# A vision transformer's tower on one core: attention contexts between a pair's two projections, value products ahead of the second pair, the shared expert's last unit in a third pair of banks, the merge behind three units

## The chip, the cores and the metric

The kernel runs on one core of a Trainium2 chip. Its engines are TensorE (PE, matrix products and transpositions into PSUM banks), VectorE (DVE), ScalarE (ACT), GpSimd (POOL) and SyncE (SP, which issues most transfers). Each follows its own instruction stream, and they meet at semaphores. The metric is the device time of one execution in microseconds (us), the median of three runs.

## The reference

The input is 16 images of 3x96x96, in float32 throughout. Cut to what matters:

```python
def tower(x):                                  # 16 images
    h = embed(x)                               # 36 patches of 16x16 -> 256, a class token, positions: (16, 37, 256)
    h = h + attention(layernorm(h))            # 16 heads of 64, relative position bias, softmax, w_o
    h = h + moe(layernorm(h))
    h = h + gated_scan(layernorm(h))           # s = (1 - d) s + d v with d = sigmoid(...), over the 37 tokens
    h = h + channel_mix(layernorm(h))          # sigmoid(xr W_r) * (relu(xk W_k)^2 W_v)
    return h

def attention(x):
    q, k, v = heads(x @ w_q), heads(x @ w_k), heads(x @ w_v)
    p = softmax(q @ k.T + bias)                # 37 x 37 for each image and head, no scaling
    return merge_heads(p @ v) @ w_o

def moe(x):                                    # 592 tokens, 7 experts of hidden width 1024
    top_vals, top_idx = top_k(x @ router_w.T, 2)
    combine = scatter(one_hot(top_idx) * softmax(top_vals))
    routed = [ (silu(x @ wg[e]) * (x @ wu[e])) @ wd[e] for e in range(7) ]
    shared = (silu(x @ swg) * (x @ swu)) @ swd
    return sum(combine[:, e] * routed[e]) + shared
```

## The kernel before, in words

**Layout.** The 592 tokens lie transposed, features on the 128 partitions, in two chunks (k) for the 256 features and two column halves (c) of 296 tokens, 8 images each. A product in nearly full float32 precision is three matmuls in a reduced type, high times high, low times high and high times low (`three`, L1673 to L1675). ACT makes the high part of an operand by a copy, DVE (`sub`, L1107) or POOL the low part by a subtraction. A product of 256 features for one column half and 128 outputs is thus 6 matmuls.

**Orders.** Every engine's order is written out by hand as one sequence of calls, and each call waits for semaphores by counts: `q_mm`/`k_mm` to `q_ev`/`k_ev` for projections and their copies, `sc_mm` to `sc_ev` for scores, `ctx_*` for contexts, `gate_mul` for multiplied hidden units, `dn_mm` for down products. PSUM banks are given by number; a writer waits until the last reader of the bank is through.

**Attention.** It goes over 8 pairs of heads; half t = 2p + c is pair p on images of column half c. Per half PE computes the scores of 8 images and 2 heads (L1809, 16 float32 matmuls, which the trace shows as 32), DVE adds the bias and takes the maxima (L1198, L1205), POOL subtracts them (`shift_scores`, L588), ACT takes the exponentials (L797), DVE sums and inverts (L1216, L1218), POOL normalises (L593), PE transposes the probabilities (`turn_probs`, L1824), ACT copies them (L792), and PE multiplies with the values (`contexts`, L1844), whose high and low parts ACT and DVE make (`context_high` L801, `context_low` through L1107). `project(p, c, j)` is a query (j = 0) or key (j = 1) projection, copied by ACT (`q_evac` L774, `k_evac` L782). In step p of the loop PE goes: scores of pair p, transpositions of pair p - 1, both projections of pair p + 1, contexts of pair p - 1, where a projection is the query or the key for both chunks of one column half. Values are five groups of token columns (`value(g, n)`, `v_evac` by ACT L749 or DVE L1165), part of which SP moves to other partitions by DMAs (L431). In step 0 there are no contexts; its place is taken by value groups 2 to 4, with the two projections of pair 1 among them.

Meanwhile SP fills buffers in DRAM (`fill_rows`, L474) and loads the experts' weights (`load`, L468), each behind a count of `sc_ev`.

**Shared expert.** It has 12 front units (FRONT), each 128 hidden features for one column half, and 4 back units that run ahead of the merge at the end of the MoE. A front unit is 12 matmuls of gate and up into the bank pair 0/1 or 2/3 by turns (`gate_up`), ACT's silu (L856), DVE's multiply (L1361), high and low parts (L863, L1107), and 12 down matmuls into banks that hold 8 units' sum for column half 0 and then 4 for half 1. Routing (top 2, places in the experts' lists) runs on DVE and POOL beside them, and POOL scatters rows by indirect DMAs (L621). `add_shared` (L1350) adds the down sums of a column half. Between the last two units PE transposes the gathered rows of expert 1 (`turn_rows`, L1965).

**Routed experts and merge.** Experts 1 to 7 take 224 gathered slots each (matmuls of 224 columns). The last one's output is scaled per slot into a high part (ACT L989) and a low part (DVE L1506), while fetched rows are weighted and summed (`scale_second` ACT L925, `weigh` DVE L1419). `merge(c)` (PE L2121 to L2129) multiplies the two parts by one-hot matrices and adds the weighted rows by an identity, each pair into one bank. The back units stand around it: two, `merge(0)`, the third, and so on, with `back_silu` (L914), `back_mul` (L1408), `back_high` (L919) on ACT and DVE.

Layer 1 (the gated scan and the channel mix) follows and is not touched.

## Time and profile before

| | |
|---|---|
| time, median of 3 runs | 312.22 us (310.87, 315.06, 312.22) |
| profiled execution's own time | 311.95 us |
| its span | 310.1 us |
| granted PE clock | 0.999 of full speed |
| PE busy, weight loads | 297.9 us (96%), 277.5 us (89%) |
| DVE, ACT, POOL busy | 189.7, 187.1, 158.1 us |

Times in the trace count from the span's start. Matmuls overlap, and their ends are modelled, so a row's busy time is longer than the step to the next one's start. The start of a row is firm; a gap between starts beyond the usual step is time that PE stood still, whether or not the row says idle. In brackets behind a row stand the idle time before it and what ended it.

### The profile page before, as it was taken

How to read it: one execution, taken by the hardware profiler on the slowest of the kernel's cores; microseconds unless marked ns; L12 is line 12 of the kernel's file. 1: busy time of each engine (PE TensorE's matmuls, PEld its weight loads, DVE VectorE, ACT ScalarE, POOL GpSimd, SP SyncE). 2: the span in 40 equal slices, each digit the busy share in tenths (PEclk: the TensorE clock that was granted, in tenths of full speed). 3: DMA queues.
4: the chain of work that ended last, by engine and by line, in shares of the span. 5: the costliest groups of instructions: out<-in, count | busy, mean ns of one | idle time of the engine just before them, and what ended most of it. 6: DMA issues, size and time to landing. Idle time of an engine off the chain costs nothing.

```text
span 310.1 us, 7379 instructions
## 1 busy us (share of the span) xinstructions
PE 297.9 (96%) x3082; PEld 277.5 (89%) x3082; DVE 189.7 (61%) x367; ACT 187.1 (60%) x326; POOL 158.1 (51%) x144
## 2 busy tenths in 40 slices
PE   8999998997999999999999999999999998999895
PEld 8877887996999999989999999999999998986673
DVE  2694445654645878467828775665748495746862
ACT  4485335774636793357697566657576463578661
POOL 7043613674535131746868495867685885100333
PEclk9999999999999999999999999999999999999999
DMA  7969343652422421669583838384856642000002
GB/s 260 406 161 232 63 113 96 206 159 71 139 61 77 128 95 48 212 188 284 171 267 127 264 117 285 107 285 147 269 169 235 200 156 87 22 2 2 1 0 82
DMA packets 32432, 46.49 MB, mean 150 GB/s; under 512 B 6965, under 2 KB 18837, under 8 KB 32394
## 3 DMA queue, kind: packets, MB, share of 16 engines
q1 hardware_dynamic: 29994, 42.16, 43.6%
q0 software_dynamic: 960, 2.43, 2.3%
q10 hardware_dynamic: 1440, 1.38, 1.5%
q8 instruction: 26, 0.43, 0.6%
q14 instruction: 12, 0.10, 0.1%
HBM read 38.22 MB, written 5.71 MB: 142 GB/s over the span
## 4 chain that ended last, share of the span: by engine, by line
PE 82%; DVE 8%; ACT 3%; issue 2%; DMA 2%; another core or an unknown queue 1%; SPq 0%; ACTq 0%; POOL 0%; DVEq 0%; POOLq 0%
PE ps L1673 20%; PE ps L1675 20%; PE ps L1674 19%; PE ps L2055 6%; PE ps L1844 3%; PE ps L1695 3%; PE ps L1824 2%; PE ps L1688 2%; DMA v_region<-v_region 2%; PE ps L1809 1%; PE ps L1681 1%; PE ps L1703 1%; DVE c_region L1107 1%; DVE w_lo L1107 1%
## 5 line engine op out<-in xcount | busy, mean ns | idle before, releaser
L1673 PE MATMUL ps<-c_region,w_hi 128*128 128x224 f32 (+2 forms) x304 | 88.2, 290 | 0.8 <-DVE c_region L1107 0.8
L1675 PE MATMUL ps<-c_region,w_lo 128*128 128x224 f32 (+2 forms) x304 | 85.4, 281 | 0.0
L1674 PE MATMUL ps<-c_region,w_hi 128*128 128x224 f32 (+2 forms) x304 | 85.2, 280 | 0.0
L565 POOL TENSOR_TENSOR w_lo<-w_stage,w_hi 128x512 fp32r<-128x512 f32 x30 | 48.6, 1638 | 34.1 <-ACT w_hi L834 34.0
L1673 PEld LDWEIGHTS ps<-c_region,w_hi 128*128 128x128 f32 x304 | 58.1, 191 | 1.6 <-DVE c_region L1107 1.0
L1674 PEld LDWEIGHTS ps<-c_region,w_hi 128*128 128x128 f32 x304 | 58.1, 191 | 0.3
L1675 PEld LDWEIGHTS ps<-c_region,w_lo 128*128 128x128 f32 x304 | 58.1, 191 | 0.0
L834 ACT ACTIVATE w_hi<-w_stage 128x1024 fp32r<-128x1024 f32 (+1 forms) x42 | 49.7, 1195 | 2.6 <-DVE v_region L1519 2.6
L1107 DVE TENSOR_TENSOR c_region<-s_region,c_region 128x448 fp32r<-128x448 f32 (+1 forms) x44 | 37.4, 851 | 17.5 <-ACT c_region L961 11.6
L572 POOL TENSOR_TENSOR w_lo<-w_stage,w_hi 128x512 fp32r<-128x512 f32 x28 | 38.0, 1389 | 8.2 <-ACT w_hi L834 8.2
L1673 PE MATMUL ps<-xn_split,w_hi 128*128 128x296 f32 x128 | 39.8, 311 | 0.6 <-DVE xn_split L1107 0.4
L1675 PE MATMUL ps<-xn_split,w_lo 128*128 128x296 f32 x128 | 38.2, 298 | 0.0
L1674 PE MATMUL ps<-xn_split,w_hi 128*128 128x296 f32 x128 | 38.2, 298 | 0.0
L1675 PE MATMUL ps<-w_hi,c_region 128*112 128x256 f32 (+2 forms) x120 | 34.6, 288 | 0.0
L1674 PE MATMUL ps<-w_lo,c_region 128*112 128x256 f32 (+2 forms) x120 | 34.5, 288 | 0.0
L1673 PE MATMUL ps<-w_hi,c_region 128*112 128x256 f32 (+2 forms) x120 | 34.5, 288 | 0.0
L1107 DVE TENSOR_TENSOR w_lo<-w_stage,w_hi 128x1024 fp32r<-128x1024 f32 x24 | 32.7, 1362 | 1.4 <-ACT w_hi L713 1.1
L961 ACT ACTIVATE c_region<-s_region 128x448 fp32r<-128x448 f32 x28 | 16.2, 578 | 20.2 <-DVE s_region L1467 19.4
L1467 DVE TENSOR_TENSOR s_region<-s_region,ps 128x448 f32<-128x448 f32 x28 | 17.2, 615 | 17.5 <-ACT s_region L956 17.1
L1673 PEld LDWEIGHTS ps<-xn_split,w_hi 128*128 128x128 f32 x128 | 24.2, 189 | 1.5 <-issue 0.6
L1674 PEld LDWEIGHTS ps<-xn_split,w_hi 128*128 128x128 f32 x128 | 24.1, 189 | 0.1
L1675 PEld LDWEIGHTS ps<-xn_split,w_lo 128*128 128x128 f32 x128 | 24.2, 189 | 0.0
(183 smaller groups left out, 565.5 us busy)
## 6 DMA issues: line engine op xcount, KB each, us to landing
w_stage<-in_w_gate SPq DMA_DIRECT2D x17, 512.0 KB, 4.3
w_stage<-in_w_up SPq DMA_DIRECT2D x17, 512.0 KB, 4.5
w_stage<-in_w_down SPq DMA_DIRECT2D x7, 1024.0 KB
expert_rows<-blank_rows SPq DMA_DIRECT2D x4, 448.0 KB, 5.1
v_region<-in_blocks SPq DMA_DIRECT2D x6, 272.0 KB, 4.1
w_stage<-in_w_down SPq DMA_DIRECT2D x3, 512.0 KB
v_region<-expert_rows SPq DMA_DIRECT2D x1, 1344.0 KB, 8.6
expert_out<-v_region ACTq DMA_DIRECT2D x6, 224.0 KB, 4.0
```

Of the source, the lines that this page charges most:

```text
L565: w = g.tensor_tensor(wl[:, r], ws[:, r], wh[:, r].bitcast(F32), ALU.subtract)
L572: w = g.tensor_tensor(wl[:, r], ws[:, r], wh[:, r].bitcast(F32), ALU.subtract)
L834: a.activation(piece(wh, n, rows), piece(ws, n, rows), ACT.Copy).then_inc(hi_e[n], 1)
L961: a.activation(gh_h[:, i * G:(i + 1) * G], prod_g[:, (i % 2) * G:(i % 2 + 1) * G], ACT.Copy).then_inc(s["g_hi"], 1)
L1107: return v.tensor_tensor(o, x, hi.bitcast(F32), ALU.subtract)
L1467: v.tensor_tensor(pat(prod_g, (i % 2) * G, [SLOTS, 2], [1, SLOTS]), pat(silu_g, (i % 2) * G, [SLOTS, 2], [1, SLOTS]), pat(bank(2 * (i % 2) ...
L1673: mm(o, a_h, b_h, start=start, stop=False)
L1674: mm(o, a_h, b_l, start=False, stop=False)
L1675: return mm(o, a_l, b_h, start=False, stop=stop)
L1695: w = mm(var_bank(L, c), ones[:], sq[:, k * N + c * NC:k * N + (c + 1) * NC], start=(k == 0), stop=(k == KD - 1))
L1844: w = mm(ps[64 * hd:64 * hd + 64, b0 + b, o:o + T], v_all[k_, vo + hd * DH:vo + (hd + 1) * DH], ptb[k_, po:po + T], start=True, stop=True)
L2055: w = mm(o, last_w(w_i, k, m), x[:, k * width + o0:k * width + o0 + NC], start=(k == 0), stop=(k == KD - 1))
```

## The change

Nothing is added to or taken from the arithmetic. The orders, the waits and some banks change:

- In steps 1 to 6 of the attention loop both contexts of pair p - 1 stand between the two column halves of pair p + 1's projections, and no longer behind the second half. `q_evac` and `k_evac` of that second half stand behind both `context_high` on ACT.
- The first column half of pair 1's projections is computed beside pair 0's, in banks 4 and 5, and all value groups 2, 3 and 4 stand ahead of the second half. Their copies are spread between the exponentials (ACT) and the sums (DVE). On POOL the low half of the query weights' later columns goes behind pair 0's two `shift_scores`.
- SP's fills and first down-weight loads wait for `k_ev` at 8, 10, 12, 14 and 16 in place of `sc_ev` at 6, 8, 10, 12 and 14.
- Unit 10 of the shared expert goes to banks 6 and 7, and unit 11 to banks 0 and 1. PE then transposes expert 1's rows (now into bank 2) and runs the down products of units 8 to 11 together. ACT and DVE take two pieces of expert 1's weights ahead of unit 8, and DVE's two adds stand behind the low parts.
- `merge(0)` stands behind three back units, and inside it the wait for the weighted rows (`mixed`) stands behind the one-hot products. ACT's first two `back_silu` and DVE's first two `back_mul` move ahead.

```diff
...
-    return bank(0, G) if e == 1 else pat(bank(4), D, [512, KD], [1, SLOTS])
+    return bank(2, G) if e == 1 else pat(bank(4), D, [512, KD], [1, SLOTS])
...
+def unit_bank(u):
+    return (6, 0)[u - FRONT + 2] if u >= FRONT - 2 else 2 * (u % 2)
...
-    return 4 if n == 1 else 6
+    return 4 if n == 2 else 6
...
     load("g0", 0)
-    sp.wait_ge(s["sc_ev"], 6)
+    sp.wait_ge(s["k_ev"], 8)
...
     load("u0", 0)
-    sp.wait_ge(s["sc_ev"], 8)
+    sp.wait_ge(s["k_ev"], 10)
...
     load("g1", 0)
-    sp.wait_ge(s["sc_ev"], 10)
+    sp.wait_ge(s["k_ev"], 12)
...
     for i in range(2):
-        sp.wait_ge(s["sc_ev"], 12 + 2 * i)
+        sp.wait_ge(s["k_ev"], 2 * HP - 2 + 2 * i)
...
-    for p in (2, 1, 0):
+    def columns_low(p):
...
+    columns_low(2)
+    columns_low(1)
...
         shift_scores(2 * p + 1)
+        if p == 0:
+            columns_low(0)
...
-    def q_evac(n):
+    def q_evac(n, done=None):
         hp, c = n // 2, n % 2
-        act.wait_ge(s["q_mm"], n + 1)
+        act.wait_ge(s["q_mm"], (n if done is None else done) + 1)
...
-    for n in range(2):
-        q_evac(n)
-        k_evac(n)
+    q_evac(0)
+    k_evac(0)
+    q_evac(2, 1)
+    q_evac(1, 2)
+    k_evac(1)
+    k_evac(2)
...
-    q_evac(2)
+    v_evac(2)
     exponentials(0)
-    k_evac(2)
+    v_evac(3)
     exponentials(1)
-    v_evac(2)
-    v_evac(3)
+    v_evac(4)
...
     k_evac(3)
-    v_evac(4)
...
             exponentials(2 * p + 1)
+        context_high(2 * p - 2)
+        context_high(2 * p - 1)
...
             output_high(p - 2)
-        context_high(2 * p - 2)
-        context_high(2 * p - 1)
...
             act.wait_ge(s["gate_mul"], done + (u - 1))
-        a.activation(silu_b[:, (u % 2) * NC:(u % 2 + 1) * NC], bank(2 * (u % 2), NC),
+        b = unit_bank(u) if isinstance(e, int) and e == 0 else 2 * (u % 2)
+        a.activation(silu_b[:, (u % 2) * NC:(u % 2 + 1) * NC], bank(b, NC),
...
-    for u in range(FRONT):
+    def rows_high(e):
+        act.wait_ge(s["xg_mm"], e)
+        a.activation(xg(e)[0], turned(e), ACT.Copy).then_inc(s["g_xh"], 1)
+    for u in range(KH):
...
             shared_high(u)
-        if u in (7, 8):
-            piece_high(("g0", "u0")[u - 7], 1)
+    piece_high("g0", 1)
+    piece_high("u0", 1)
+    silu(0, KH)
+    for u in range(KH + 1, FRONT):
+        silu(0, u)
+        shared_high(u - 1)
+    rows_high(1)
+    shared_high(FRONT - 1)
...
-    def rows_high(e):
-        act.wait_ge(s["xg_mm"], e)
-        a.activation(xg(e)[0], turned(e), ACT.Copy).then_inc(s["g_xh"], 1)
-    rows_high(1)
...
                                  scale=slot_w[0:SP, st:st + 1]).then_inc(s["yw_hi"], 1)
+                back_silu(0)
                 scale_second(2)
+                back_silu(1)
...
             gathered_expert(e)
-        back_silu(0)
-        back_silu(1)
...
             context_low(2 * p - 3)
-        if p < HP:
+        if p == 0:
+            v_evac(2)
+            sums(0)
+            v_evac(3)
+            sums(1)
+            v_evac(4)
+        elif p < HP:
...
             sums(2 * p + 1)
-        if p == 0:
-            for g in (2, 3, 4):
-                v_evac(g)
...
     rank_experts(0, TA)
-    for u in range(FRONT):
+    def shared_mul(u):
...
             dve.wait_ge(s["hid_lo"], u - 1)
-        v.tensor_tensor(prod_b[:, r], silu_b[:, r], bank(2 * (u % 2) + 1, NC),
+        v.tensor_tensor(prod_b[:, r], silu_b[:, r], bank(unit_bank(u) + 1, NC),
                         ALU.mult).then_inc(s["gate_mul"], 1)
+    for u in range(KH):
+        shared_mul(u)
...
             late_rows()
-        if u == 8:
-            piece_low("g0", 1)
-        if u == 10:
-            dve.wait_ge(s["dn_mm"], KH)
-            add_shared(0, s["acc_ok"])
-            add_shared(1, s["acc_ok"])
+    piece_low("g0", 1)
+    shared_mul(KH)
+    for u in range(KH + 1, FRONT):
+        shared_mul(u)
+        shared_low(u - 1)
...
     rows_low(1)
+    shared_low(FRONT - 1)
     piece_low("g1", 1)
+    dve.wait_ge(s["dn_mm"], KH)
+    add_shared(0, s["acc_ok"])
+    add_shared(1, s["acc_ok"])
...
                                            op1=ALU.subtract).then_inc(s["yw_lo"], 1)
+                back_mul(0)
                 weigh(2)
-                back_mul(0)
+                back_mul(1)
...
-        back_mul(1)
...
         n = 2 * hp + c
-        if n >= 2:
+        if n not in (0, 2):
...
             project(0, c, j)
+        project(1, 0, c)
...
         hp, half = t // 2, t % 2
-        pe.wait_ge(s["q_ev"], t + 1)
+        pe.wait_ge(s["q_ev"], 3 if t == 1 else t + 1)
...
         if p + 1 < HP:
-            project(p + 1, 0, 0)
-            project(p + 1, 0, 1)
             if p == 0:
-                for g in (2, 3):
+                for g in (2, 3, 4):
...
                         value(g, n)
+            else:
+                project(p + 1, 0, 0)
+                project(p + 1, 0, 1)
+                contexts(2 * p - 2)
+                contexts(2 * p - 1)
...
             project(p + 1, 1, 1)
-            if p == 0:
-                for n in range(2):
-                    value(4, n)
...
             output(1, 0, 0, 4)
-        if p >= 1:
...
         c, j = unit(u) if shared else (u // KH, u % KH)
-        if not (shared and u < 2):
-            pe.wait_ge(s["gate_mul"], u - 1 if shared else e * 16 + (u - 1 - BACK))
+        if not shared:
+            pe.wait_ge(s["gate_mul"], e * 16 + (u - 1 - BACK))
+        elif u == FRONT - 2:
+            pe.wait_ge(s["xt_ok"], 3)
+            pe.wait_ge(s["count_set"], 1)
+        elif u >= 2:
+            pe.wait_ge(s["gate_mul"], u - 2 if u == FRONT - 1 else u - 1)
+        b = unit_bank(u) if shared else 2 * (u % 2)
...
                 x_ = slice(k * NT + c * NC, k * NT + (c + 1) * NC)
-                w = three(bank(2 * (u % 2) + q, NC), wh[:, w_], wl[:, w_], xh[:, x_], xl[:, x_],
+                w = three(bank(b + q, NC), wh[:, w_], wl[:, w_], xh[:, x_], xl[:, x_],
...
             pe.wait_ge(s["d_x1"], 16)
-            pe.wait_ge(s["gate_mul"], FRONT - 1)
+            pe.wait_ge(s["gate_mul"], FRONT - 2)
...
             for st in range(ST):
-                o = bank(0, SP, k * SLOTS + st * SP) if e == 1 else bank(4 + k, SP, D + st * SP)
+                o = bank(2, SP, k * SLOTS + st * SP) if e == 1 else bank(4 + k, SP, D + st * SP)
...
             pe.wait_ge(lo_e["dn"], 1)
-        if u == KH + 2:
-            pe.wait_ge(s["xt_ok"], 3)
-            pe.wait_ge(s["count_set"], 1)
-        if u == FRONT - 1:
-            turn_rows(1)
-        down(0, u - 2, first=u - 2 in (0, KH))
+        if u < FRONT - 2:
+            down(0, u - 2, first=u == 2)
...
             turn_tokens(u - 3)
-    down(0, FRONT - 2)
-    down(0, FRONT - 1)
+    turn_rows(1)
+    pe.wait_ge(s["gate_mul"], FRONT - 1)
+    for u in range(KH, FRONT):
+        down(0, u, first=u == KH)
...
             pe.wait_ge(s["yw_lo"], ST)
-            pe.wait_ge(s["mixed"], TT if c else 3)
...
                     mm(bank(o, NC), yw_l[0:SP, y_], hot(st, c)[0:SP, :], start=False, stop=False)
-                t, k0, k1, at = PART[c]
-                mm(bank(o, k1 - k0, at), back0[:, t * D + m * P:t * D + (m + 1) * P], ident[:, k0:k1],
+            pe.wait_ge(s["mixed"], TT if c else 3)
+            t, k0, k1, at = PART[c]
+            for m in range(KD):
+                mm(bank(4 + 2 * c + m, k1 - k0, at), back0[:, t * D + m * P:t * D + (m + 1) * P], ident[:, k0:k1],
...
         back_gate_up(1)
+        back_gate_up(2)
         merge(0)
-        back_gate_up(2)
...
```

Three places of the orders. The first is PE in the attention loop, at the end of the second half's key projection and what follows, up to the scores of the next pair (`ps` is a PSUM bank; one float32 matmul here is two in the trace). Before:

```order
L1673 MATMUL ps<-xn_split,w_hi 128x296 [waits k_ev]
L1674 MATMUL ps<-xn_split,w_hi 128x296
L1675 MATMUL ps<-xn_split,w_lo 128x296
L1673 MATMUL ps<-xn_split,w_hi 128x296
L1674 MATMUL ps<-xn_split,w_hi 128x296
L1675 MATMUL ps<-xn_split,w_lo 128x296
L1844 MATMUL ps<-probs_T,v_region 64x37 [waits ctx_lo,pt_ev]
L1844 MATMUL ps<-probs_T,v_region 64x37 x15
L1844 MATMUL ps<-probs_T,v_region 64x37 [waits pt_ev]
L1844 MATMUL ps<-probs_T,v_region 64x37 x15
L1809 MATMUL ps<-k_buf,q_buf 37x37 [waits sc_ev,k_ev,q_ev]
L1809 MATMUL ps<-k_buf,q_buf 37x37 x15
```

And now:

```order
L1697 MATMUL ps<-xn_split,w_hi 128x296 [waits k_ev]
L1698 MATMUL ps<-xn_split,w_hi 128x296
L1699 MATMUL ps<-xn_split,w_lo 128x296
L1697 MATMUL ps<-xn_split,w_hi 128x296
L1698 MATMUL ps<-xn_split,w_hi 128x296
L1699 MATMUL ps<-xn_split,w_lo 128x296
L1834 MATMUL ps<-k_buf,q_buf 37x37 [waits sc_ev,k_ev,q_ev]
L1834 MATMUL ps<-k_buf,q_buf 37x37 x15
L1834 MATMUL ps<-k_buf,q_buf 37x37 [waits k_ev,q_ev]
L1834 MATMUL ps<-k_buf,q_buf 37x37 x15
```

The 32 context matmuls no longer stand between the key projection and the scores that read its copy.

The second place is DVE at the end of the shared units (multiply, low part, weight pieces, the two adds). Before:

```order
L1361 TENSOR_TENSOR s_region<-s_region,ps 128x296 [waits hid_lo,hid_hi,silu_ok]
L1107 TENSOR_TENSOR c_region<-s_region,c_region 128x296 [waits dn_mm,hid_hi]
L1107 TENSOR_TENSOR w_lo<-w_stage,w_hi 128x2x512 [waits hi_g0]
L1361 TENSOR_TENSOR s_region<-s_region,ps 128x296 [waits hid_lo,hid_hi,silu_ok]
L1107 TENSOR_TENSOR c_region<-s_region,c_region 128x296 [waits dn_mm,hid_hi]
L1361 TENSOR_TENSOR s_region<-s_region,ps 128x296 [waits hid_lo,hid_hi,silu_ok]
L1107 TENSOR_TENSOR c_region<-s_region,c_region 128x296 [waits dn_mm,hid_hi]
L1350 TENSOR_TENSOR hT<-hT,ps 128x296 [waits dn_mm]
L1350 TENSOR_TENSOR hT<-hT,ps 128x296
L1361 TENSOR_TENSOR s_region<-s_region,ps 128x296 [waits hid_lo,hid_hi,silu_ok]
L1107 TENSOR_TENSOR c_region<-s_region,c_region 128x296 [waits dn_mm,hid_hi]
L1107 TENSOR_TENSOR c_region<-ps,c_region 128x448 [waits g_xh]
```

And now:

```order
L1122 TENSOR_TENSOR w_lo<-w_stage,w_hi 128x2x512 [waits hi_g0]
L1379 TENSOR_TENSOR s_region<-s_region,ps 128x296 [waits hid_lo,hid_hi,silu_ok] x2
L1122 TENSOR_TENSOR c_region<-s_region,c_region 128x296 [waits dn_mm,hid_hi]
L1379 TENSOR_TENSOR s_region<-s_region,ps 128x296 [waits hid_lo,hid_hi,silu_ok]
L1122 TENSOR_TENSOR c_region<-s_region,c_region 128x296 [waits dn_mm,hid_hi]
L1379 TENSOR_TENSOR s_region<-s_region,ps 128x296 [waits hid_lo,hid_hi,silu_ok]
L1122 TENSOR_TENSOR c_region<-s_region,c_region 128x296 [waits dn_mm,hid_hi]
L1122 TENSOR_TENSOR c_region<-ps,c_region 128x448 [waits g_xh]
L1122 TENSOR_TENSOR c_region<-s_region,c_region 128x296 [waits dn_mm,hid_hi]
L1122 TENSOR_TENSOR w_lo<-w_stage,w_hi 128x2x512 [waits hi_g1]
L1368 TENSOR_TENSOR hT<-hT,ps 128x296 [waits dn_mm]
L1368 TENSOR_TENSOR hT<-hT,ps 128x296
```

The weight piece moved ahead of unit 8's multiply, each multiply now precedes the low part of the unit before, and the adds went to the end.

The third place is DVE ahead of the merge (yw low parts, weighted row, back units). Before:

```order
L1506 SCALAR_TENSOR_TENSOR c_region<-ps,softmax_stats,c_region 112x256 [waits yw_hi,slot_ok,g_y]
L1506 SCALAR_TENSOR_TENSOR c_region<-ps,softmax_stats,c_region 112x256 [waits yw_hi]
L1419 SCALAR_TENSOR_TENSOR v_region<-v_region 128x256 [waits r_scaled,d_back2]
L1408 TENSOR_TENSOR s_region<-probs_T,ps 128x296 [waits b_silu]
L1107 TENSOR_TENSOR w_lo<-w_stage,w_hi 128x1024 [waits hi_dn]
L1408 TENSOR_TENSOR s_region<-probs_T,ps 128x296 [waits b_silu]
```

And now:

```order
L1530 SCALAR_TENSOR_TENSOR c_region<-ps,softmax_stats,c_region 112x256 [waits yw_hi,slot_ok,g_y]
L1530 SCALAR_TENSOR_TENSOR c_region<-ps,softmax_stats,c_region 112x256 [waits yw_hi]
L1432 TENSOR_TENSOR s_region<-probs_T,ps 128x296 [waits b_silu]
L1443 SCALAR_TENSOR_TENSOR v_region<-v_region 128x256 [waits r_scaled,d_back2]
L1432 TENSOR_TENSOR s_region<-probs_T,ps 128x296 [waits b_silu]
L1122 TENSOR_TENSOR w_lo<-w_stage,w_hi 128x1024 [waits hi_dn]
```

The first back unit's multiply now stands ahead of `weigh`, the second right behind it.

## Rows read from the trace of the kernel before

**Rows 1.** The page, parts 1 and 3: busy time, and PE's instruction queue

```profile
PE 297.9 (96%) x3082; PEld 277.5 (89%) x3082; DVE 189.7 (61%) x367; ACT 187.1 (60%) x326; POOL 158.1 (51%) x144
...
q8 instruction: 26, 0.43, 0.6%
```

**Rows 2.** Table of waits, PE: total us, times, longest us

```profile
PE ps L1824 <- issue: 2.6, 1, 2.6
```

**Rows 3.** Timeline of PE, pair 0: start, us, line, operation, [idle before <-releaser]

```profile
27.52 0.30 PE L1675 MATMUL ps<-xn_split,w_lo 128*128 128x296 f32 x1
28.21 0.41 PE L1673 MATMUL ps<-xn_split,w_hi 128*128 128x296 f32 x1 [0.39 <-DVE xn_split L1107]
...
30.05 0.49 PE L1809 MATMUL ps<-k_buf,q_buf 64*37 64x37 f32 x32
30.72 0.49 PE L1809 MATMUL ps<-k_buf,q_buf 64*37 64x37 f32 x32 [0.18 <-ACT k_buf L782]
31.14 0.41 PE L1673 MATMUL ps<-xn_split,w_hi 128*128 128x296 f32 x1
```

**Rows 4.** Timeline of ACT, the same stretch

```profile
30.16 0.42 ACT L782 ACTIVATE k_buf<-ps 128x296 f32<-128x296 f32 x1 [0.39 <-PE ps L1675]
```

**Rows 5.** Timeline of PE, steps 4 and 5 of the loop

```profile
62.63 0.82 PE L1809 MATMUL ps<-k_buf,q_buf 64*37 64x37 f32 x64
63.38 1.02 PE L1824 MATMUL ps<-consts,s_region 101*111 101x101 f32 x8
64.18 0.38 PE L1673 MATMUL ps<-xn_split,w_hi 128*128 128x296 f32 x1
...
67.61 1.14 PE L1844 MATMUL ps<-probs_T,v_region 37*64 37x37 f32 x64
68.56 0.82 PE L1809 MATMUL ps<-k_buf,q_buf 64*37 64x37 f32 x64
71.96 0.99 PE L1824 MATMUL ps<-consts,s_region 101*111 101x101 f32 x8 [2.58 <-issue]
```

**Rows 6.** Timeline of DVE, the same stretch

```profile
63.51 0.47 DVE L1198 TENSOR_TENSOR s_region<-ps,bias_pair 101x296 f32<-101x296 f32 x1 [1.85 <-PE ps L1809]
...
65.26 0.83 DVE L1107 TENSOR_TENSOR c_region<-ps,c_region 128x296 fp32r<-128x296 f32 x2
```

**Rows 7.** Windows: length, PE, PEld, DVE, ACT, POOL busy, clock, DMA share, GB/s

```profile
67.40:69.40 2.00, 1.98 (x131) 1.70 (x129) 0.19 (x1) 1.52 (x4) 1.50 (x3) 1.00 0.56 186
69.40:70.60 1.20, 0.00 (x0) 0.00 (x0) 1.13 (x3) 0.14 (x1) 0.72 (x2) 1.00 0.06 17
```

**Rows 8.** DMA queues from 69.40 to 70.60: packets, MB, share

```profile
q8 instruction: 1, 0.02, 4.8%
```

**Rows 9.** Timelines of DVE and PE, values and contexts of pair 0

```profile
43.19 0.69 DVE L1165 COPY v_region<-ps 128x512 f32<-128x512 f32 x1 [3.70 <-PE ps L1675]
...
48.24 0.67 PE L1844 MATMUL ps<-probs_T,v_region 37*64 37x37 f32 x32
50.27 0.67 PE L1844 MATMUL ps<-probs_T,v_region 37*64 37x37 f32 x32 [1.36 <-DMA v_region<-v_region]
```

**Rows 10.** Timelines of ACT and PE, end of the shared units

```profile
131.94 0.42 ACT L856 ACTIVATE s_region<-ps 128x296 f32<-128x296 f32 x1 [2.47 <-PE ps L1675]
...
132.90 0.41 PE L1673 MATMUL ps<-xn_split,w_hi 128*128 128x296 f32 x1 [0.19 <-issue]
...
140.09 0.40 PE L1673 MATMUL ps<-c_region,w_hi 128*128 128x296 f32 x1 [0.76 <-DVE c_region L1107]
...
141.02 0.34 PE L1673 MATMUL ps<-c_region,w_hi 128*128 128x224 f32 x1
```

**Rows 11.** Timelines of ACT, DVE and PE ahead of the merge

```profile
262.14 0.84 ACT L989 ACTIVATE c_region<-ps,softmax_stats 112x256 fp32r<-112x256 f32 x2 [4.31 <-remote]
...
262.74 0.88 DVE L1506 SCALAR_TENSOR_TENSOR c_region<-ps,softmax_stats,c_region 112x256 fp32r<-112x256 f32 x2 [3.77 <-ACT c_region L989]
...
264.16 0.37 PE L2121 MATMUL ps<-xn_split,c_region 112*128 112x296 f32 x1 [1.38 <-DVE v_region L1419]
```

## The prediction, made from the rows of the kernel before alone

> **What bounds the kernel now.** I read the page first: the tensor engine (PE) is busy 297.9 of 310.1 us [rows 1], so only what PE waits for can move the time. Next the table of waits, which puts PE's largest idle time ahead of a transposition of the probabilities, 2.6 us with no releaser [rows 2]; the next, 1.38 us, is ahead of the merge [rows 11]. Since the ends of matmuls are modelled, I then took the starts of PE's instructions in the timeline: projection matmuls start every 0.14 us, and a longer step is a stall even where it reads as busy. So read, these are what the change can reach: 0.55 us at 28.21 (0.69 us after the start before it, not 0.14) [rows 3]; about 0.34 us in pair 0, where 64 score matmuls take 30.05 to 31.14 = 1.09 us against 62.63 to 63.38 = 0.75 us later [rows 3, 5]; 1.57 us between the contexts of pair 0's halves, 48.24 to 50.27 (half of 64 take 0.48) [rows 9]; 2.58 us at 69.38 to 71.96; 0.76 us and more at the end of the shared units [rows 10]; 1.5 us before the merge [rows 11]. All else runs packed, at a granted clock of 1.00 [rows 7].
>
> **The attention loop.** No matmul is added. The contexts of the pair before move from behind the second projections to between the first and the second. In a packed loop that saves nothing; what matters is which covers go.
>
> (1) The key projection of a pair is now followed at once by the next pair's scores. Their first half needs old buffers only, their second half this projection's copy by ACT. Pair 0 of the old kernel has exactly this order: projection ends, first scores at 30.05, ACT copies k 30.16 to 30.58 [rows 4], second scores 30.72. So the second half starts 0.67 us after the first and not 0.33: +0.34 us. Before, 0.95 us of contexts (67.61 to 68.56) hid that copy. It now comes ahead of pairs 1 to 7. Pair 1's is counted in (4): 6 x 0.34 = +2.0 us. Bounds: 0.18 (what the row itself calls idle) and 0.40 each, 1.1 to 2.4.
>
> (2) The contexts write banks that DVE must have read for the pair before (the low halves, L1107, awaited as ctx_lo). DVE does that at 65.26 to 66.09, 2.6 us after its start at 63.51, which is 0.13 us behind the scores [rows 5, 6]. Old contexts started at 67.61, 1.5 us later. Counted from the first scores T: scores now end T+1.09, DVE starts T+1.22 and is done T+3.80; PE has transpositions (0.80) and two projections (64.18 is 0.80 after 63.38; half of 64.18 to 67.61 = 1.7) behind it and stands ready at T+3.6 to 3.7. It waits 0.2 us, and one more change between kinds of matmul costs 0.08 (64.18 starts a matmul that takes 0.22 to the next). 5 pairs (2 to 6) x 0.28 = +1.4 us; bounds 0 (DVE starts behind the first half) and 0.5 each, 0 to 2.5. Queued behind the waiting contexts are the second projections and the next scores, so it is paid in full.
>
> (3) The stall at 69.38. Nothing that PE waits for is late: it stands with no releaser. In the 1.2 us from 69.40 PE does nothing, the data queues nearly stop (DMA share 0.56, then 0.06) [rows 7], and one packet of PE's instruction queue moves [rows 8]. That queue moved 26 packets in all for 3082 matmuls and as many weight loads [rows 1]: 237 instructions each. Contexts and scores back to back, 67.61 to 69.38, are 128 matmuls and 128 loads, over one packet's worth in 1.77 us. I read it as the instruction stream running dry where this stretch met a packet's edge while a fill of expert_rows and a weight load held the queues. Two projections now stand inside the stretch (1.6 us, and 0.34 of wait), and the fills are issued behind the pair's last copy and not with the load. I take -2.3 us of the 2.58; bounds 0 and -2.58.
> By the Trainium skill's page "Runtime: NRT & Kernel Launch", section "Instruction fetch mechanics", the crossing of a 16 KiB block is mostly hidden, since dispatch is slower than the fill. By that rule the stall is no fetch and has no reason to leave, and the sum below would be 313.6. The row of 2.58 us with no releaser speaks against "hidden"; the rule stands as rival B.
>
> (4) Pairs 0 and 1. A first projection of pair 1 in each column half fills the 0.55 us at 28.21 and covers the copy of pair 0's keys (0.34). All three value groups now run ahead of pair 1's second projections, so the last value copy (43.19 to 43.88 [rows 9]) comes some 2 us earlier, and with it the two transfers behind it, which let the contexts go at 50.27. But the contexts wait earlier too, by 1.6 us. I give that wait 0.35 us back (bounds 0 and 1.57), 0.2 for the transpositions that waited for the last value copy, take 0.4 off because group 3 needs a gather whose issue does not move, and 0.34 off for pair 1's scores. Sum -0.7, less 0.2 for changes of kind: -0.5 us; bounds +0.3 and -1.8.
>
> ACT and DVE have the same instructions per pair. POOL's part of the query weights goes behind two shifts; its readers are the projections of pairs 4 to 7. SP's fills wait for k_ev in place of sc_ev, most of a pair later; what they and the loads behind them bring is read only behind the loop. All that costs nothing as long as PE's loop stays the longest.
>
> **The shared units.** Old: ACT takes unit 8's silu at 131.94 though its matmuls ended near 129.5, and ends up behind; the last multiply stands behind the two adds, so the last down matmuls start 140.09 with 0.92 us lost (0.76 of it idle), and 0.35 us goes ahead of 132.90 [rows 10]. New: unit 10 goes to banks 6 and 7, so unit 11 follows with no wait, the four last down groups go together, and the adds stand behind. Even with silu 8 at 131.94: units 10 and 11 end 136.0, the rows' transposition follows (4 matmuls, 0.3), four down groups of 0.81 end at 139.7; the last low half is ready by 138.6 (silu 11 at 136.15, then 0.42, 0.46, 0.45, rows 0.53, then 0.50, with the handovers). Expert 1 starts 139.75 and not 141.02: -1.25 us; bounds 0 (the wait is only passed on) and -1.3 (all of it). The experts behind show no idle PE, so it is kept.
>
> **The merge.** A third back unit goes ahead of it. But it reuses banks 0 and 1, so it needs back_mul(0), which needs back_silu(0), which stands behind ACT's scaled copies. They start only at 262.14 [rows 11]. Then ACT 0.84, DVE's two low parts to 263.62, back_mul(0) to 264.1: the unit starts at 264.15, and the merge started at 264.16. The cause, the late copy, stays; only the last link changes. I take 0, bounds +0.4 and -1.5.
>
> **Sum** against the profiled execution's 311.95 us: -0.5 +2.0 +1.4 -2.3 -1.25 +0 = -0.65, so 311.3. The median of the three runs is 312.22, 0.27 above; I forecast **311.4 us**, that is, no difference that can be told.
>
> **Rivals.** A, as summed: 0.42, own range 310.2 to 312.8. B, the other side: the instruction stall stays or strikes at another edge, while waits (1) and (2) come. It decides at a packet's edge near the first contexts of pair 4 or 5. 311.4 + 2.3 = 313.7, slower than before; for it: the fetch needs some 2.5 to 4 us (71.96 - 67.61 = 4.35 at most) and the new stretch lasts only 3.7; 0.22. C, the waits do not come (DVE starts sooner, ACT's copy is hidden): 311.4 - 3.4 = 308.0; against it pair 0's rows; 0.14. D, the merge's wait of 1.5 us is hidden because ACT's copies come early: 309.9; 0.10. E, the end of the units gains nothing (a late silu of a later unit): 312.6; 0.07. Left over 0.05.
>
> The range from **307.8 to 314.8** holds A to E and the bounds of (1) to (4) around B and C. 2% of 312.22 is 6.2 us, about what a measurement here can tell from none: faster by that would need every stall gone and no new wait, 0.04; slower would need stalls of over 6 us, 0.03.
>
> **What would show it.** In the new trace: second scores 0.67 us behind the first in pairs 1 to 7, idle for ACT's k_buf (1); contexts of pairs 2 to 6 released by DVE L1122 or by nothing late, pair period 6.5 us against 5.9 (2); no idle without releaser in the loop (3); values over by 41.2 (4); expert 1's first matmul 1.2 us earlier relative to unit 0; back unit 2 idle some 1.4 us for DVE's multiply in place of the merge. I am wrong if the loop's period stays at 5.9, or if PE idles with no releaser in the loop.

## The result, and the profile of the changed kernel

The changed kernel takes **314.81 us** (median of 20 runs, 313.57 to 316.43), the kernel before 312.22 us in as many. The ratio of the runs is **1.0071, 95% interval 1.0048 to 1.0095**: slower, by less than the 2% line. Repeated later it gave 1.0095 [1.0059, 1.0131]. I had forecast 311.4 us and no change that can be told, with a range that ends at 314.8.

The profiled execution took 313.57 us. The page, its span and busy times, against [rows 1]:

```profile
span 311.8 us, 7378 instructions
PE 300.8 (96%) x3082; PEld 278.9 (89%) x3082; DVE 187.7 (60%) x367; ACT 187.4 (60%) x326; POOL 157.5 (51%) x144
```

The same matmuls, 2.9 us more in which PE reads as busy. The table of waits (total us, times, longest) says what PE waits for:

```profile
PE ps L1869 <- DMA v_region<-v_region: 1.3, 1, 1.3
PE ps L1697 <- DVE s_region L1432: 1.2, 1, 1.2
PE ps L1834 <- ACT k_buf L791: 1.1, 6, 0.2
...
PE ps L1869 <- DVE c_region L1122: 0.8, 5, 0.2
PE ps L1995 <- DMA v_region<-expert_rows: 0.7, 1, 0.7
```

The 2.6 us with no releaser [rows 2] are gone. In their place stand six waits for the key copy and five for DVE's low half (in steps 2 to 6), and the two ends of the MoE wait for something else than before. One step of the loop, timeline of PE, against [rows 5]:

```profile
58.91 1.02 PE L1849 MATMUL ps<-consts,s_region 101*111 101x101 f32 x8
59.71 0.38 PE L1697 MATMUL ps<-xn_split,w_hi 128*128 128x296 f32 x1
...
61.76 1.14 PE L1869 MATMUL ps<-probs_T,v_region 37*64 37x37 f32 x64 [0.17 <-DVE c_region L1122]
62.83 0.40 PE L1697 MATMUL ps<-xn_split,w_hi 128*128 128x296 f32 x1
...
64.66 0.49 PE L1834 MATMUL ps<-k_buf,q_buf 64*37 64x37 f32 x32
65.33 0.49 PE L1834 MATMUL ps<-k_buf,q_buf 64*37 64x37 f32 x32 [0.18 <-ACT k_buf L791]
```

The second scores start 0.67 us behind the first, as pair 0's did [rows 3]. ACT's copy and DVE's low half, which release the two waits:

```profile
64.77 0.42 ACT L791 ACTIVATE k_buf<-ps 128x296 f32<-128x296 f32 x1 [0.40 <-PE ps L1699]
```

```profile
60.78 0.83 DVE L1122 TENSOR_TENSOR c_region<-ps,c_region 128x296 fp32r<-128x296 f32 x2
```

The loop's period, from transposition to transposition, is 6.85 us against 5.93. Inside it, by the starts: scores 1.09 us (0.75 before), first projections and what follows up to the contexts 2.05, contexts 1.07 (0.95), second projections 1.84; both projections together took 3.43.

At the end of the shared units and ahead of the merge, against [rows 10] and [rows 11], PE again:

```profile
139.22 0.60 PE L1995 MATMUL ps<-consts,v_region 112*128 112x112 f32 x4 [0.73 <-DMA v_region<-expert_rows]
...
265.76 0.41 PE L1697 MATMUL ps<-xn_split,w_hi 128*128 128x296 f32 x1 [1.24 <-DVE s_region L1432]
```

Where the 1.6 us between the two profiled executions come from, by the starts of equal matmuls: ahead of the loop +0.2 (noise of the start); pairs 0 and 1 up to the transpositions of step 2 +0.3; steps 2 to 6 **+2.0**, which is 5 x 0.92 = +4.6 less the stall's 2.65; shared units -0.6; the experts and the stretch around the merge -0.3.

### The profile page after: what moved, and what is told of

It is laid out like the page before. It is cut to its first block, busy times and chain, and to the rows that moved or that the text cites. A ratio compares the mean times of both kernels' runs of the same rounds, so it can differ in the third digit from the quotient of the medians.

```text
span 311.8 us, 7378 instructions
## 1 busy us (share of the span) xinstructions
PE 300.8 (96%) x3082; PEld 278.9 (89%) x3082; DVE 187.7 (60%) x367; ACT 187.4 (60%) x326; POOL 157.5 (51%) x144
## 3 DMA queue, kind: packets, MB, share of 16 engines
q10 hardware_dynamic: 1440, 1.38, 1.6%
## 4 chain that ended last, share of the span: by engine, by line
PE 72%; DVE 11%; DMA 5%; issue 4%; ACT 3%; POOL 2%; another core or an unknown queue 1%; SPq 1%; ACTq 0%; DVEq 0%; POOLq 0%
PE ps L1697 17%; PE ps L1699 17%; PE ps L1698 17%; PE ps L2083 6%; PE ps L1869 3%; PE ps L1719 3%; DVE c_region L1122 2%; PE ps L1712 2%; DMA v_region<-v_region 2%; POOL expert_rows L630 2%; DVE s_region L1213 2%; PE ps L1727 1%; PE ps L1705 1%; DMA c_region<-xn_split 1%
## 5 line engine op out<-in xcount | busy, mean ns | idle before, releaser
L569 POOL TENSOR_TENSOR w_lo<-w_stage,w_hi 128x512 fp32r<-128x512 f32 x30 | 47.3, 1597 | 33.1 <-ACT w_hi L844 33.1
L1122 DVE TENSOR_TENSOR c_region<-s_region,c_region 128x448 fp32r<-128x448 f32 (+1 forms) x44 | 37.2, 847 | 15.2 <-ACT c_region L976 11.6
L576 POOL TENSOR_TENSOR w_lo<-w_stage,w_hi 128x512 fp32r<-128x512 f32 x28 | 38.0, 1389 | 8.9 <-ACT w_hi L844 8.9
L1697 PE MATMUL ps<-w_hi,c_region 128*112 128x256 f32 (+2 forms) x120 | 34.5, 287 | 0.4 <-DMA c_region<-xn_split 0.4
L1122 DVE TENSOR_TENSOR w_lo<-w_stage,w_hi 128x1024 fp32r<-128x1024 f32 x24 | 31.6, 1317 | 2.0 <-ACT w_hi L722 1.1
```

Of the source, the lines that this page charges most:

```text
L569: w = g.tensor_tensor(wl[:, r], ws[:, r], wh[:, r].bitcast(F32), ALU.subtract)
L576: w = g.tensor_tensor(wl[:, r], ws[:, r], wh[:, r].bitcast(F32), ALU.subtract)
L1122: return v.tensor_tensor(o, x, hi.bitcast(F32), ALU.subtract)
L1697: mm(o, a_h, b_h, start=start, stop=False)
```

## The experiments

Experiments one to four, five to eight and nine to twelve ran on three different chips, each time with the kernel before beside them. Its median was 311.5, 308.7 and 312.4 us there, so ratios are compared, and traces segment by segment. Most kernels here have a single profile. "By the starts" means from one instruction's start to the next one's.

**One: the contexts behind again.** The changed kernel, the contexts put back on PE and ACT:

```diff
                         project(p + 1, 0, 0)
                         project(p + 1, 0, 1)
-                        contexts(2 * p - 2)
-                        contexts(2 * p - 1)
                     project(p + 1, 1, 0)
                     project(p + 1, 1, 1)
+                    if p >= 1:
+                        contexts(2 * p - 2)
+                        contexts(2 * p - 1)
```

> The changed kernel with one thing undone: in steps 1 to 6 both contexts stand behind the second half's projections again, on PE and in ACT's order. Theory T: each loop step of the change pays 0.34 us for the copy of the keys, 0.33 us for the wait on DVE's low half and 0.24 us for two more changes between kinds of matmul; so the period falls from 6.85 to 5.93 us, and no stall without a releaser comes back, since it went with the later fills: profiled time 313.6 - 5 x 0.92 - 0.6 = 308.4. Rival F (the stall belongs to contexts and scores back to back at the edge of PE's instruction packets): period 5.93 in all steps but one, which has the 2.6 us stall again: 311.0. Rival N (the loss is not in the loop): no change, 313.6.

308.42 us, ratio 0.9893 [0.9852, 0.9933]. The period is back at 5.93 us; the placement of the contexts alone turns a faster kernel into a slower one. But PE stands again with no releaser ahead of the same transpositions, for 1.2 us:

```profile
67.23 0.84 PE L1834 MATMUL ps<-k_buf,q_buf 64*37 64x37 f32 x64
69.26 0.99 PE L1849 MATMUL ps<-consts,s_region 101*111 101x101 f32 x8 [1.18 <-issue]
```

The total met theory T by luck: pairs 0 and 1 gained more than it said, and the stall, which it had gone, came back at less than half of rival F's 2.6 us.

**Two: the contexts alone.** The kernel before with only the contexts moved, on PE and ACT (the diff above, turned round).

> The kernel before with one thing changed: the contexts between the two halves' projections in steps 1 to 6. Theory T: period 6.85 us in place of 5.93, and as the fills are issued as early as before, the stall without a releaser stays: 312.0 + 5.2 = 317.2. Rival F (the stall needs contexts and scores back to back): the stall goes, 314.6. Rival N: within 0.5 us of before.

318.51 us, ratio 1.0249 [1.0196, 1.0302]: slower. The loop has the waits of the changed kernel; the stall shrinks to 0.6 us but stays. The profiled execution took 317.34 us, which meets theory T's 317.2 by luck: it loses 2.0 us less at the stall, and 1.7 more in pair 0, whose contexts wait twice as long for the values' transfer, since they come earlier and the values do not (and the granted clock falls to 0.50 behind that wait, see the last section):

```profile
50.18 0.67 PE L1844 MATMUL ps<-probs_T,v_region 37*64 37x37 f32 x32 [3.01 <-DMA v_region<-v_region]
```

**Three: the fills alone.**

```diff
-            sp.wait_ge(s["sc_ev"], 6)
+            sp.wait_ge(s["k_ev"], 8)
             fill_rows(1)
...
```

> The kernel before with one thing changed: SP's fills and first down-weight loads wait for the key copies and not for the scores' readers. If the stall at 69.38 is a matter of what the queues carry at that moment: it goes, 309.4. Rival F (it is a matter of the matmuls' order at a packet's edge) : it stays, 312.0, at the same matmul.

Ratio 1.0010 [0.9973, 1.0048]: nothing. The stall is at the same matmul with 1.18 us in place of 2.58:

```profile
72.94 0.99 PE L1824 MATMUL ps<-consts,s_region 101*111 101x101 f32 x8 [1.18 <-issue]
```

I took this at first for an effect of the fills; experiments six and twelve say otherwise. Twelve has 1.2 us with the fills where they were.

**Four: low halves first on DVE.** In the changed kernel:

```diff
             for p in range(HP + 2):
+                if p >= 2:
+                    context_low(2 * p - 4)
+                    context_low(2 * p - 3)
                 if p < HP:
...
-                if p >= 2:
-                    context_low(2 * p - 4)
-                    context_low(2 * p - 3)
```

> The changed kernel with DVE's low halves of the contexts ahead of the bias additions of the next pair and not behind them. Theory T: the contexts' wait for ctx_lo (0.33 us in each of 5 steps) goes, period 6.52, 313.6 - 1.7 = 311.9. Rival: the bias additions come 0.8 us later, so the transpositions or the scores' buffers wait in place of the contexts, and the time stays at 313.6.

313.61 us, ratio 1.0051 [1.0016, 1.0086], against 1.0071 and 1.0095 of the changed kernel: too near to tell by time, and not theory T's 311.9. The trace tells: no wait for ctx_lo, and the period from contexts to contexts is 6.60 us in place of 6.85, so the wait cost 0.25 (not 0.33). The 5 x 0.25 us do not show in the total, since in this profile pair 0's contexts wait 1.95 us for the values in place of 1.34, and the granted clock falls to 0.50 for some 3 us behind that wait, as it does not in the first profile of the changed kernel.

```profile
68.68 1.14 PE L1869 MATMUL ps<-probs_T,v_region 37*64 37x37 f32 x64
...
75.28 1.14 PE L1869 MATMUL ps<-probs_T,v_region 37*64 37x37 f32 x64
```

**Five: one context between, one behind.** On top of the fourth, with ACT's context copies behind its last key copy:

```diff
                         contexts(2 * p - 2)
-                        contexts(2 * p - 1)
                     project(p + 1, 1, 0)
                     project(p + 1, 1, 1)
+                    if p >= 1:
+                        contexts(2 * p - 1)
```

> The changed kernel with the low halves first on DVE (as in the run before it) and one of a pair's two contexts between the halves' projections, the other behind the second half, with ACT's context copies behind its last key copy. Theory T (three separate costs): the 32 context matmuls behind the projections hide the copy of the keys (0.34 us gone from each of 5 steps), the wait for the low halves is gone too (0.24), and only the changes between kinds of matmul stay, 0.32 us over the old order: period 6.25, 313.6 - 5 x 0.6 = 310.6. Rival (the changes of kind are no cost of their own, the waits hide them): period 5.95, 309.1. Rival (the key copy is still waited for): 6.6, 312.3.

307.38 us, ratio 0.9931 [0.9900, 0.9962]. Period 6.27 us from one scores to the next (67.99 less 61.72, and the step before it too), which theory T had as 6.25: with both waits covered, 0.34 us per step stay for two changes more between contexts and projections. Inside a step the two contexts take 0.60 and 0.49 us (0.95 for both before) and the two halves' projections 1.81 and 1.82 (3.43):

```profile
61.72 0.82 PE L1834 MATMUL ps<-k_buf,q_buf 64*37 64x37 f32 x64
...
65.09 0.67 PE L1869 MATMUL ps<-probs_T,v_region 37*64 37x37 f32 x32
65.69 0.40 PE L1697 MATMUL ps<-xn_split,w_hi 128*128 128x296 f32 x1
```

The three costs add up: 5.93 + 0.34 + 0.34 + 0.25 = 6.86.

**Six: the last fill later.** The kernel of the first experiment with

```diff
-            sp.wait_ge(s["k_ev"], 12)
+            sp.wait_ge(s["k_ev"], 14)
             fill_rows(3)
```

> The kernel with the contexts behind (308.4 us, in which PE still stands 1.2 us with no releaser at its matmul 973), with one thing changed: the last fill of expert_rows is issued one step later, so none is in the queues as PE comes to that matmul. Theory Q (PE waits for a packet of its instruction queue, which queues behind the fill): the packet lands earlier and the 1.2 us go, 307.2. Rival (the packet is asked for too late whatever the queues carry): 1.2 us stay, 308.4.

306.47 us, ratio 0.9916 [0.9887, 0.9945]. SP issued the fill at 73.74, behind the stretch, and PE stood all the same:

```profile
67.12 0.82 PE L1834 MATMUL ps<-k_buf,q_buf 64*37 64x37 f32 x64
68.99 0.99 PE L1849 MATMUL ps<-consts,s_region 101*111 101x101 f32 x8 [1.05 <-issue]
```

The part of theory Q on the fill falls: the stall does not need it. The fill is not without effect, though. In the first, third and eighth experiments SP issues it 0.4 to 0.5 us after the start of PE's instruction packet; the packet takes 1.2 to 1.3 us there and 0.9 here, and PE goes on 2.8 us after its start and 2.3 here. But here the packet also starts 0.4 us later against PE's stream.

**Seven: the stream shifted.**

```diff
             keep_clock(9)
+            for _ in range(40):
+                mm(bank(3, 16), zero[:], zero[:, 0:16], start=True, stop=True)
```

> The kernel before with 80 small matmuls more (as the trace counts) at its start, so that PE's stream of instructions is shifted by 80 matmuls against the program. Theory Q: the stall with no releaser stays at about matmul 973 of the trace, which is now in the scores or contexts of the step before the old place, or vanishes because the stretch ahead of it is another; it does not stay at the transpositions behind the same scores. Rival (the place in the program makes it, a bank or a semaphore there): it stays ahead of the same transpositions, now matmul 1053 to 1055, with 2.6 us. The time itself grows by the added matmuls, some 3 us.

The stall is gone, from the transpositions and from matmul 973. The place in the program does not make it. The time, 324.48 us in one run, is far above the 3 us expected: the 80 matmuls alone take 13.8 us by the starts (last section).

**Eight: the rows' transposition behind two down groups.** The kernel of the first experiment with

```diff
-            turn_rows(1)
             pe.wait_ge(s["gate_mul"], FRONT - 1)
             for u in range(KH, FRONT):
+                if u == FRONT - 2:
+                    turn_rows(1)
                 down(0, u, first=u == KH)
```

> The kernel with the contexts behind (308.4 us), with the transposition of expert 1's rows behind the down products of units 8 and 9 and no longer ahead of all four, and ACT's and DVE's copies of the rows behind those of unit 11. Theory T: the 0.96 us that PE stands there for the transfer of the rows are covered by 1.6 us of down products, 307.6. Rival: units 8 and 9 are not ready earlier either, or the down product of unit 11 or expert 1's first product waits for its copy instead, and nothing is gained.

306.17 us, ratio 0.9883 [0.9831, 0.9936], the lowest ratio here, though its interval holds the first experiment's 0.9893. The transfer no longer holds PE, but the down products wait for the multiply of unit 10 (0.45 us by the starts, 0.29 of it idle). From the first matmul of unit 9 to that of expert 1 the trace has 9.91 us, against 10.36 in the first experiment and 10.26 in the sixth: 0.35 to 0.45 of the 0.9 us are won, the rival took the rest. In this trace PE also stands 0.53 us with no releaser once more, in pair 6's scores, matmul 1100 (see experiment twelve).

```profile
133.87 0.41 PE L1697 MATMUL ps<-c_region,w_hi 128*128 128x296 f32 x1 [0.29 <-DVE s_region L1379]
135.60 0.55 PE L1996 MATMUL ps<-consts,v_region 112*128 112x112 f32 x4
```

**Nine: pairs 0 and 1 alone.** The kernel before with only the parts of the change on `qk_bank`, the first projection of pair 1, the value groups and their copies.

> The kernel before with only the part of the change on pairs 0 and 1: pair 1's first half projected beside pair 0's in banks 4 and 5, all value groups ahead of the second half, the copies and POOL's low half as the change has them; contexts, fills, units and merge as before. Theory T: this part gives 1.7 us by itself, as the stretch from the first value products to the scores of pair 2 does in the kernel with the contexts behind (28.7 against 30.4 us); the changed kernel shows nothing of it because its contexts come earlier and wait for the same transfers. Ratio 0.9945. Rival (this part is worth the 0.5 us of the prediction, the rest comes with the later fills): 0.998.

309.41 us, ratio **0.9923** [0.9892, 0.9953]: this part is a gain by itself. From the first value products to the middle of step 2's scores the trace has 28.4 us against 30.5. Half of it is the wait of the contexts, 0.30 us where it was 1.36 [rows 9]:

```profile
48.35 0.67 PE L1854 MATMUL ps<-probs_T,v_region 37*64 37x37 f32 x32 [0.30 <-DMA v_region<-v_region]
```

**Ten: the shared units alone.** The kernel before with `unit_bank` and the orders of units 8 to 11.

> The kernel before with only the shared units' part of the change: unit 10 in banks 6 and 7, the order of units 8 to 11 and of the adds. Theory T: 0.7 us are gained between unit 5 and expert 1, as in the changed kernel, and 0.9 us of wait for the transfer of expert 1's rows stands where the wait for DVE's low half stood; ratio 0.998. Rival (the prediction's 1.25 us, the transfer's wait being made by the other parts): 0.996.

Ratio 1.0016 [0.9984, 1.0049], no gain that can be told, and less than the prediction's 1.25 us. From unit 9 to expert 1 the trace has 11.00 us against 10.91 in the first profile of the kernel before. What PE no longer waits for DVE it waits for the rows:

```profile
135.51 0.61 PE L1986 MATMUL ps<-consts,v_region 112*128 112x112 f32 x4 [1.44 <-DMA v_region<-expert_rows]
```

But the first profile of the kernel before is not typical here either. In its second one, from the chip of this experiment, and in those of the third and ninth experiments, which have the old order, the stretch takes 11.6 us: PE waits 0.9 us for DVE's multiply ahead of unit 10, besides the 0.7 later. Against these this part gains 0.6 us, and the changed kernel's two profiles (10.28, 10.65) gain 0.95 to 1.3.

**Eleven and twelve: both kernels once more.**

> The changed kernel itself, on the chip of this call. Theory T: the loop's period is 6.85 us here too, and the ratio 1.007. Where this chip is one on which ACT's scaled copies are not late, neither kernel waits ahead of the merge, both are 1.5 us shorter, and the ratio stays.

> The kernel before itself, one more profile. Theory Q (a packet of the instruction queue comes late behind the fill): the stall with no releaser is again ahead of the transpositions behind matmul 973, its length again 2.3 to 2.8 us less the lead of the packet. Rival: it is an accident of one execution and is gone. The 1.4 us ahead of the merge stay if they are the order's, and go if they are the chip's.

The changed kernel: 314.83 us, ratio 1.0095; steps 2 to 6 take 34.5 us together against 34.4, and the wait of the third back unit is 1.25 us. It too has a stall with no releaser here, 0.37 us, in pair 6's scores. The kernel before: the stall is at the same place with 1.21 us, not 2.58.

```profile
71.07 1.59 PE L1824 MATMUL ps<-consts,s_region 101*111 101x101 f32 x8 [1.21 <-issue]
```

So the 2.58 us on which I had counted were one execution's. From the records of PE's instruction queue, the start of the one packet near matmul 973, counted from 0 (against that matmul's start) and the time until matmul 974 starts:

```
kernel                    packet   974 starts   packet to 974
before, first profile      +0.38     2.77         2.39
before, again              -1.16     1.41         2.57
units only                 -1.19     1.13         2.32
values only                -1.17     1.33         2.50
fills only                 -1.41     1.39         2.80
contexts behind            -1.42     1.38         2.81
last fill later            -1.06     1.24         2.30
rows' turn later           -1.55     1.22         2.77
contexts alone             -1.67     0.81         2.48
split                      -2.18     0.31         2.49
changed, first profile     -2.61     0.13         no stall
changed, again             -2.73     0.15         no stall
low halves first           -2.71     0.13         no stall
```

In the ten profiles with a stall PE goes on 2.3 to 2.8 us after the packet's start, however they differ; where the packet leads by 2.6 us or more nothing is lost. (The split's 0.31 us is the usual 0.13 and a stall of 0.2.) The two stalls in pair 6's scores fit: PE goes on at matmul 1100, 2.38 us (rows' turn later) and 2.28 us (changed, again) after the start of the next packet. The first profile of the changed kernel passes that matmul 2.18 us after the packet's start with nothing lost, so 2.2 to 2.8 us is a range seen and no fixed time. The stretch ahead of matmul 973 is contexts and scores back to back, 128 matmuls and as many weight loads in 1.70 us, the densest kind of stretch in the program; the kernel before has one in each of five steps, and stands long at one of them. That goes with the split (which puts 12 projection matmuls into it) and the change (12 as well, and a wait) losing little or nothing, and with a shift by 80 matmuls doing away with it. All this is a relation read from profiles, and the shift; what sets the moment at which the packet starts was not found.

## Why the prediction was wrong

It said no difference and 311.4 us; it is 0.7% slower and 314.8 us. By its own steps:

- **(1) Scores wait for the key copy: right.** 6 x 0.34 = 2.0 us, to the hundredth as forecast.
- **(2) Contexts behind DVE's low half: the step that failed, in size.** 0.28 us a step was forecast, 0.59 measured. The wait was right (0.2 forecast, 0.25 by the fourth experiment). The term that was mis-sized is the change between kinds of matmul: it was taken as 0.08 us, the extra of the first projection matmul alone; the split shows 0.34. I had missed that both ends of a block of projections cost (64.18 to 64.40 at its start [rows 5], and 0.22 in place of 0.14 us to the next instruction at its end), and that contexts take 0.12 us more where projections follow than where scores do (1.07 against 0.95 us), which makes 0.28 of the 0.34. With step 1, which has the changes but not the wait, that is 6 x 0.34 + 5 x 0.25 = 3.3 us and not 1.4.
- **(3) The stall goes: right in the trace compared, too large for the runs.** 2.65 us went, 2.3 were forecast. But it was a single profile: 1.0 to 1.3 us are what the seven profiles lose there that have the old spacing and are not this one, so against a typical execution the term was too large by about 1 us. My cause was half right: it goes with the instruction stream, as the relation in the table has it. Two projections in the stretch do not do it alone: with the contexts moved and nothing else 0.6 us stay (second experiment). That the fill held the packet back is refuted by the sixth experiment, but for some 0.4 us of the packet's own time. The Trainium skill's page "Runtime: NRT & Kernel Launch", section "Instruction fetch mechanics", calls the crossing of a block mostly hidden. Most packets here cost nothing that shows either; but if the stall is such a crossing, as the table suggests, it cost 1.0 to 2.6 us at matmul 974 in the eight profiles with the old spacing. Rival B, whose loss came near the measured time, had the two waits right, but the stall did not stay in the first profile, and cost 0.3 us at another place in the second.
- **(4) Pairs 0 and 1: -0.5 forecast, about -0.35 measured** (the +0.3 up to step 2, less 0.34 for pair 2's scores and 0.34 for step 1's changes of kind). Alone this part gives 1.7 to 2.4 us (ninth experiment). The contexts of pair 0, moved ahead by about as much as the values are, wait for the same transfer as long as before:

```profile
48.53 0.67 PE L1869 MATMUL ps<-probs_T,v_region 37*64 37x37 f32 x32 [1.34 <-DMA v_region<-v_region]
```

- **Shared units: -1.25 forecast, -0.6 measured in the profiles compared, none to be told by time for this part alone.** DVE's wait went as said, but the rows' transposition, which I had costed at its four matmuls, had been covered by a unit's down products and is now first in line; I had not looked at when the rows land. Rival E had half of the result and another cause.
- **The merge: 0 forecast, about -0.1 measured,** and as said: the third unit waits 1.24 us for `back_mul(0)` where the merge waited 1.38. Rival D's condition, early copies, was met on the chip of experiments five to eight, by the kernel before as well (last section).

From the sum of -0.65 to the profiled +1.6: (2) +1.9, (3) -0.35, (4) +0.15, shared units +0.6, merge and experts -0.3, noise of the start +0.2, which makes +1.6 with the rounding. The medians lie further apart, by 2.6 us. The second profile of the kernel before has the likely reason: it lost 1.35 us less at the stall than the first, and 0.7 more ahead of unit 10, and 1.6 + 1.35 - 0.7 is 2.3. The single profile had flattered the change, in the forecast and in the comparison.

## What to carry to other kernels

Price an instruction block that is moved into another by its edges on both sides, and measure each edge from both kinds of neighbours: here the two more edges, 0.34 us a step, cost as much as the wait for the keys and more than the one for the low half. What stands between a producer and its reader is cover, even where it seems to be in the way; half of the moved block behind the projections was enough to hide the key copy (fifth experiment). And when a wait is removed, look up when the next operand in line lands before the gain is booked. A stall that one profile shows is worth a second profile: here 2.6 us became 1.2.

## What the runs showed of the hardware

**A stall can cost twice.** In the second profile of the kernel before, PE stood 1.2 us at 69.86, and then its granted clock fell to 0.50 for about 3 us. Windows view (length; PE, PEld, DVE, ACT, POOL busy; clock; DMA share; GB/s):

```profile
70.00:71.00 1.00, 0.00 (x0) 0.00 (x0) 0.97 (x3) 0.02 (x1) 0.51 (x2) 1.00 0.00 0
71.00:72.00 1.00, 0.93 (x6) 0.96 (x7) 0.96 (x3) 0.05 (x1) 0.82 (x2) 0.64 0.33 47
72.00:73.00 1.00, 1.00 (x6) 1.00 (x6) 0.50 (x2) 0.67 (x2) 0.52 (x1) 0.50 0.96 348
73.00:74.00 1.00, 1.00 (x6) 1.00 (x6) 0.00 (x0) 0.12 (x1) 0.00 (x0) 0.50 0.42 154
74.00:75.00 1.00, 1.00 (x7) 1.00 (x6) 0.00 (x0) 0.76 (x2) 0.00 (x0) 0.65 0.00 0
```

Projection matmuls went every 0.25 us there and not every 0.14; the rest of the loop took 1.6 us more than without the fall, besides the stall. 0.5 is the lower of the two levels, 1.2 GHz. The second profile of the changed kernel had the same behind the 1.4 us that its pair 0 waits for the values:

```profile
48.00:49.00 1.00, 0.57 (x32) 0.59 (x32) 0.00 (x0) 0.00 (x0) 0.69 (x1) 1.00 0.07 27
49.00:50.00 1.00, 1.00 (x13) 0.97 (x7) 0.00 (x0) 0.73 (x2) 0.00 (x0) 0.94 0.00 0
50.00:51.00 1.00, 1.00 (x6) 1.00 (x6) 0.00 (x0) 0.42 (x1) 0.00 (x0) 0.50 0.00 0
```

The same stalls left the clock alone in the first profiles of both. In five profiles the clock fell behind pair 0's wait (1.4 to 3.0 us in them), in one behind the stall; in the five in which pair 0 waits 0.3 us or not at all it did not fall. The spread of the times goes with it. Of the kernel before's 25 runs beside experiments nine to twelve, the eleven with a mean granted clock of 0.998 or more have a median of 311.1 us, the ten with 0.993 to 0.995 one of 312.8: 1.7 us, about what this one fall cost. On the chip of five to eight it is 308.5 and 310.5. And all 36 runs of experiments one, five, six and eight, where pair 0 waits 0.3 us at most, have 0.998 or more, where over a third of the runs of the kernel before beside them have less. The ninth, with the same short wait and the stall of 1.1 us, has four of 12 below. What decides whether the clock falls behind a given wait was not found.

**The clock fell over the added matmuls.** In the seventh experiment PE ran 80 matmuls of 16 columns at the start of the program, from 4.98 to 18.81 us. The first 33 started every 0.11 us, the others every 0.21 us, as the clock went from full to half, and it stayed there well into the embedding (the page, clock in 40 slices):

```profile
PEclk9569999979999999999999999999999999999999
```

The kernel before has 9 in every slice. The run was 12.5 us longer than the first profile of the kernel before, and 16 us longer than its median on that chip. The added matmuls are 13.8 us of that, some 9 of which they would take every 0.11 us and some 5 the half clock added; the embedding behind them lost another 1.5 us to it.

**The wait ahead of the merge is not the kernel's alone.** On the chips of experiments one to four and nine to twelve, and in the first profiles, ACT's scaled copies start 2.9 us after the start of the last matmul that they read (263.85 against 260.98 in the changed kernel), and on that of five to eight 0.3 us after it, and then PE has no wait there and the three traces of the changed order are 1.5 us shorter at that place. The same holds for the silu of unit 8 in the old order: it starts 2.8 to 3.5 us after the unit's last matmul on the other chips, and 0.3 us after it in the seventh experiment, where PE then has no wait ahead of unit 10. The two are worth 1.5 us and 0.2 to 0.9 us of the 2.6 by which the kernel before is faster on that chip (308.5 against 311.1 us at a granted clock of 0.998 or more), and part of what the change gains at the shared units exists only where ACT is late. Whether the chip or something in it makes this is open.
